# A tanh-attention kernel: softmax denominators as four 32-column products, and a new order of VectorE's steps behind them

## The reference

```python
def proj(W, bias):
    y = jnp.tanh(states @ W + bias)
    return y.reshape(b, s, h, d).transpose(0, 2, 1, 3)     # h = 16 heads, d = 64
q, k, v = (proj(Wq, bq), proj(Wk, bk), proj(Wv, bv))
alpha = jnp.einsum('bhqd,bhkd->bhqk', q, k) / jnp.sqrt(jnp.float32(d))
causal = jnp.tril(jnp.ones((s, s), dtype=bool))
alpha = jnp.where(causal, alpha, jnp.finfo(jnp.float32).min)
alpha = jax.nn.softmax(alpha, axis=-1)
ctx = jnp.einsum('bhqk,bhkd->bhqd', alpha, v)
ctx = ctx.transpose(0, 2, 1, 3).reshape(b, s, h * d)
return jnp.tanh(ctx @ Wo + bo)
```

## Time and profile before

| | |
|---|---|
| median of 3 runs | 1631.6 us (1628.72 to 1643.32) |
| the profiled execution | 1633.24 us, its span 1631.4 us |
| busy: TensorE | 1551.1 us (95%) |
| busy: VectorE | 1419.4 us (87%) |
| busy: ScalarE | 1227.8 us (75%) |
| busy: GpSimd | 461.1 us (28%) |
| mean granted TensorE clock | 0.991 of full |

### The profile page before, as it was taken

One profiled execution on the slowest core, in us unless ns is written; L12 is line 12 of the kernel. 1 busy time (PEld: TensorE's weight loads), 2 busy tenths in 40 slices (PEclk: granted clock), 3 DMA queues, 4 the chain that ended last, 5 costly groups with the idle time before them and its releaser, 6 DMA issues.

```text
span 1631.4 us, 38607 instructions
## 1 busy us (share of the span) xinstructions
PE 1551.1 (95%) x14806; PEld 701.8 (43%) x14806; DVE 1419.4 (87%) x2102; ACT 1227.8 (75%) x1698; POOL 461.1 (28%) x563
## 2 busy tenths in 40 slices
PE   7899999999999999998899999999999999989996
PEld 4344444444444444445333333333333333466774
DVE  6777778888888888998899999999999999397888
ACT  4667666677666676664798999899989999666776
POOL 3311112222333323334135242324332432120004
PEclk9999999999999999999999999999999999899998
DMA  5311001111011110001112000200030000000001
GB/s 146 73 39 40 30 30 40 39 37 39 21 39 39 37 39 34 26 3 33 34 41 53 15 14 15 53 14 15 19 82 19 15 28 2 1 8 8 14 14 52
DMA packets 46606, 52.98 MB, mean 32 GB/s; under 512 B 9279, under 2 KB 33551, under 8 KB 46482
## 3 DMA queue, kind: packets, MB, share of 16 engines
q1 hardware_dynamic: 45584, 50.05, 10.5%
q10 hardware_dynamic: 898, 1.22, 0.3%
HBM read 15.07 MB, written 10.49 MB: 16 GB/s over the span
## 4 chain that ended last, share of the span: by engine, by line
PE 63%; DVE 22%; ACT 10%; issue 3%; POOL 1%; ACTq 0%; POOLq 0%; DVEq 0%
DVE arena L2408 16%; PE psum L590 15%; PE psum L571 12%; ACT arena L2164 7%; PE psum L1916 5%; PE psum L533 5%; PE psum L1547 5%; PE psum L1514 4%; PE psum L608 3%; PE psum L1927 3%; PE psum L628 3%; PE psum L1902 1%; PE psum L553 1%; PE psum L554 1%; PE psum L555 1%
## 5 line engine op out<-in xcount | busy, mean ns | idle before, releaser
L2408 DVE TENSOR_REDUCE arena<-psum 128x2 f32<-128x1024 f32 x490 | 565.7, 1214 | 11.1 <-PE psum L1927 9.8
L2164 ACT ACTIVATE arena<-psum 128x512 f32<-128x512 f32 x980 | 519.6, 600 | 52.0 <-PE psum L1902 46.1
L755 ACT ACTIVATE arena<-psum 128x2048 f32<-128x2048 f32 (+1 forms) x160 | 274.0, 1713 | 229.0 <-PE psum L571 228.9
L1916 PE MATMUL psum<-arena 128*32 128x256 f32 x4096 | 329.2, 393 | 1.4 <-ACT arena L2184 0.2
L859 POOL TENSOR_SCALAR_AFFINE_SELECT arena<-arena 128x512 f32<-128x512 f32 (+1 forms) x160 | 152.7, 972 | 508.7 <-ACT arena L755 508.7
L590 PE MATMUL psum<-arena,hs 128*64 128x512 f32 (+3 forms) x1536 | 283.0, 496 | 0.2 <-POOL arena L859 0.2
L1902 PE MATMUL psum<-arena 32*128 32x512 bf16 x1024 | 255.9, 385 | 1.3 <-ACT arena L2164 0.4
L571 PE MATMUL psum<-arena 64*128 64x512 f16 (+3 forms) x2304 | 215.0, 324 | 2.1 <-DVE arena L907 1.6
L1927 PE MATMUL psum<-arena 32*128 32x512 bf16 x980 | 189.9, 384 | 21.0 <-DVE arena L2408 13.1
L907 DVE TENSOR_TENSOR arena<-arena 128x1024 f16<-128x1024 f32 x64 | 78.4, 1226 | 101.4 <-ACT arena L734 101.4
L590 PEld LDWEIGHTS psum<-arena,hs 128*64 128x64 f32 x1536 | 95.9, 136 | 141.5 <-issue 125.2
(11 more groups left out here) (222 smaller groups left out, 2160.1 us busy)
## 6 DMA issues: line engine op xcount, KB each, us to landing
arena<-arena SPq DMA_DIRECT2D x30, 512.0 KB, 2.9
arena<-arena SPq DMA_DIRECT2D x46, 128.0 KB, 2.2
arena<-latent_q SPq DMA_DIRECT2D x64, 64.0 KB, 2.0
arena<-latent_k SPq DMA_DIRECT2D x64, 64.0 KB, 2.0
arena<-arena SPq DMA_DIRECT2D x60, 64.0 KB, 2.2
X<-in_L_attn_states SPq DMA_DIRECT2D x4, 512.0 KB, 4.4
latent_q<-arena SPq DMA_DIRECT2D x16, 96.0 KB, 2.3
latent_k<-arena SPq DMA_DIRECT2D x16, 96.0 KB, 2.3
```

Of the source, the lines that this page charges most:

```text
L755: nc.scalar.activation(probs[g], SC[:, :, 0:WIDTH[g]], ACT.Exp, scale=DH ** -0.5).then_inc(exp_done, 1)
L1916: last = nc.tensor.matmul(OT[ROWS * c:ROWS * (c + 1), h * HALF // 2:(h + 1) * HALF // 2], v_cols[par][:, kt, 2 * pr + i, :], e_probs[u % 4 ...
L2164: nc.scalar.activation(e_probs[u % 4][:, i * HALF:(i + 1) * HALF], ring(n, u, i), ACT.Exp, scale=KD ** -0.5).then_inc(e_done, 1)
L2408: nc.vector.tensor_reduce(half_tops[:, kh, qt, 2 * pr:2 * pr + 2], src.rearrange("p (i c) -> p i c", i=2), AX.X, ALU.max).then_inc(top_don ...
```

## The change

- `denominators`: each of the four products (head s, half of the queries) takes 32 columns of `ones` and writes a group of 32 partitions of its own, all at the same 512 columns of PJ. The semaphore is raised once, by 2, behind the last.
- `read_denominators`: one transpose of 512 columns in place of two.
- `invert`: writes the inverses of a group of partitions into both halves of `rden_col`.
- `share` (new): four copies of 32 partitions x 16 elements bring to each head's other group of partitions the inverses that it lacks.
- VectorE's order: `add_output(i-2)` now stands ahead of `share` and `spread(i-1)`, where `spread` stood between the first and the second addition of group 3.
- denT is half as long.

```diff
--- before.py
+++ after.py
@@ -366,7 +366,7 @@
         qk_end = a1b.at
         assert qk_end == SUMS_AT
         sums = [a1b.take(2 * S).rearrange("p (s q) -> p s q", s=2) for _ in range(2)]
-        denT = a1b.take(S)
+        denT = a1b.take(HALF)
         rden_col = a1b.take(S // 32)
         ctxT = [a1b.take(S) for _ in range(2)]
         ctx_hi = [a1b.take(S // 2, F16) for _ in range(2)]
@@ -397,6 +397,8 @@
         tile_tanh, tile_stats, tile_pow, tile_normed, tile_added, tile_reset = (
             sem("tile_tanh"), sem("tile_stats"), sem("tile_pow"), sem("tile_normed"), sem("tile_added"), sem("tile_reset"))
         PAIR_DMAS = 3
+        QB = HALF // 32
+        INVERSE = 6
         SUM_LO, SUM_HI = 4, 7
 
         NORM_FROM = PAIRS + 2
@@ -602,12 +604,12 @@
                     pe.wait_ge(tanh_done, 4 * (n + 2) + 4)
                 pe.wait_ge(sum_lo, SUM_LO * (n + 1))
                 pe.wait_ge(sum_hi, SUM_HI * (n + 1))
-                for half in range(2):
-                    now = slice(half * HALF, (half + 1) * HALF)
-                    for s in range(2):
-                        last = nc.tensor.matmul(PJ[s * DH:(s + 1) * DH, now], ones, sums[par][:, s, now],
-                                                start=True, stop=True, skip_group_check=True)
-                    last.then_inc(den_done, 1)
+                for c in range(4):
+                    s, half = c // 2, c % 2
+                    last = nc.tensor.matmul(PJ[ROWS * c:ROWS * (c + 1), 0:HALF], ones[:, 0:ROWS],
+                                            sums[par][:, s, half * HALF:(half + 1) * HALF],
+                                            start=True, stop=True, skip_group_check=True)
+                last.then_inc(den_done, 2)
 
             def output(n, par):
 
@@ -921,24 +923,32 @@
 
             def read_denominators(n):
 
-                for half in range(2):
-                    dve.wait_ge(den_done, 2 * n + half + 1)
-                    now = slice(half * HALF, (half + 1) * HALF)
-                    nc.vector.transpose(denT[:, now], PJ[:, now]).then_inc(den_read, 1)
+                dve.wait_ge(den_done, 2 * n + 2)
+                nc.vector.transpose(denT, PJ[:, 0:HALF]).then_inc(den_read, 2)
 
             def invert(n):
                 dve.wait_ge(den_read, 2 * n + 2)
-                nc.vector.reciprocal(rden_col, denT.rearrange("p (b c) -> p b c", c=32)[:, :, 0]).then_inc(rden_ready, 1)
+                v = denT.rearrange("p (b c) -> p b c", c=32)[:, :, 0].unsqueeze(1).to_broadcast([P, 2, QB])
+                nc.vector.reciprocal(rden_col.rearrange("p (h b) -> p h b", h=2), v).then_inc(rden_ready, 1)
+
+            def share(n):
+
+                dve.wait_ge(rden_ready, INVERSE * n + 1)
+                for c in range(4):
+                    half, other = c % 2, c ^ 1
+                    now = slice(half * QB, (half + 1) * QB)
+                    nc.vector.tensor_copy(rden_col[ROWS * other:ROWS * (other + 1), now], rden_col[ROWS * c:ROWS * (c + 1), now]
+                                          ).then_inc(rden_ready, 1)
 
             def spread(n):
-                dve.wait_ge(rden_ready, 2 * n + 1)
+                dve.wait_ge(rden_ready, INVERSE * n + 5)
                 if not at_least(n, 1):
                     dve.wait_ge(wo_split, 3)
                 nc.vector.transpose(rden.rearrange("p (b c) -> p b c", c=32),
                                     rden_col.unsqueeze(2).to_broadcast([P, S // 32, 32])).then_inc(rden_ready, 1)
 
             def scale_ctx(n, par):
-                dve.wait_ge(rden_ready, 2 * n + 2)
+                dve.wait_ge(rden_ready, INVERSE * (n + 1))
                 dve.wait_ge(out_copied, n + 1)
                 nc.vector.tensor_tensor(ctxT[par], ctxT[par], rden, ALU.mult).then_inc(ctx_scaled, 1)
 
@@ -1039,14 +1049,15 @@
                     states_lo(dve, 1, PJ)
                     state_moments(dve, 3)
                 hi_third(i, par, 0)
-                if at_least(i, 1):
-                    spread(i - 1)
                 hi_third(i, par, 1)
                 hi_third(i, par, 2)
                 if at_least(i, 2):
                     add_output(i - 2)
                 else:
                     states_lo(dve, 2 + i, PJ)
+                if at_least(i, 1):
+                    share(i - 1)
+                    spread(i - 1)
                 if norm:
                     norm_tile(t)
                     add_tile(t)
@@ -1090,6 +1101,7 @@
             read_denominators(N1 - 1)
             invert(N1 - 1)
             quads_ahead(dve, 2, 3)
+            share(N1 - 1)
             spread(N1 - 1)
             scale_ctx(N1 - 1, 1)
             quads_ahead(dve, 3, 4)
```

## The result

| | before | changed |
|---|---|---|
| median (20 runs each) | 1632.95 us (1628.13 to 1643.32) | 1642.78 us (1635.47 to 1646.97) |
| ratio, 95% interval | | 1.0052 (1.0037 to 1.0067) |
| profiled span | 1631.4 us | 1641.0 us |

The changed kernel is slower than before, by half a per cent, and outside the range of the prediction. Over all executions of before that ran beside the experiments, the median is 1628.6 us at a mean clock of 0.995 (12 executions) and 1639.4 at 0.986 (22).

A forecast was written before the change was run, and what follows sets the result against it. TensorE looked busiest, but GpSimd's mask, then VectorE's scaling, would limit the gain. Terms -3.8 + 4.0 - 1.2 - 1.3 = -2.3 took the profiled 1633.24 to 1630.9 us, 1629 us as median; range 1617 to 1640 us.

The forecast's parts named there:

- Four products beside each other: TensorE's denominators: four products run concurrently instead of two and two, shrinking the stage by 0.82 us.
- What of it counts: the mask: TensorE's context 3 then waits for GpSimd's mask, so gains are 0.48 us per early pair (3.8 us), 0.1 us later.
- Output added first: VectorE's output addition starts at about 324.3 instead of 325.59; the values' wait goes, returning late pairs to 22.30 us.
- 0.1 us for uncertainty: Late pairs: allowance for the uncertain start of VectorE's output addition, added to the rounding's start.
- What is late next: VectorE's scaling comes after addition, copies and spreading; ScalarE's context rounding waits for it, with 0.79 us spare before.
- X, the four copies: VectorE's four copies of inverses, 32 x 16 elements each: taken as 0.7 us, between 0.3 and 0.85 us.
- The first mask in the way: GpSimd's group 0 mask goes ahead of VectorE's scaling and delays it by 0.45 us.
- The sum of the late pairs: Pairs 10 to 30: period 22.65 us against 22.45, +4.0 us over twenty pairs, bounds -5 to +11 us.
- the spare behind the rounding: ScalarE, from context rounding to the queries' tanh that releases TensorE's next projection: about 0.1 us of spare.
- Pair 1: TensorE's wait for L228 shortens as the transpose moves and the product shrinks: -1.2 us, bounds 0 and -1.9.
- The end: Last denominators: shorter product stage and earlier addition, less 0.7 us for copies: -1.3 us in all, bounds 0 and -2.5.
- The rival that called it (scaling becomes the bound, 1636 us): Late pairs: copies plus mask make scaling the bound, 23.0 us a pair, 1636 us; chance of slower 0.15.

The follow-up runs named there:

- the run with the mask in two: Changed kernel with context 3 waiting only for the first pass of group 3's mask, its last key tile for the second: 1626.19 us, ratio 0.9956.
- the order alone: Kernel before with only the spreading transpose moved behind the output's addition, two-and-two products, no copies: 1626.49 us, ratio 0.996.
- the old products in the cured order: Changed kernel with scaling ahead of tile steps, context 3's mask wait split, and all 32 pairs' denominators as before, no copies: 1628.99 us, ratio 0.9982.

## Why the prediction was wrong, and where it was right

Forecast 1629.0 us, no change, range 1617 to 1640; measured 1642.78. By its own steps:

- *Four products beside each other.* Right: 1.06 us instead of 1.89, 0.83 saved (0.82 worked out).
- *What of it counts: the mask.* Right. Early pairs gained 3.7 us over eight (3.8), context 3 waits 0.49 us for the mask, and the run with the mask in two takes the wait away. With it early pairs run at 21.58 us, 0.72 under before, so 0.1 us of the 0.82 is held by something else.
- *Output added first.* Right in kind: the values' wait is gone, and the order alone brings the late period to 22.31 (22.30). The addition starts later than I gave it: 0.2 to 0.3 us behind the output's end (320.20 against 318.38 + 1.51 = 319.89), of which 0.17 is "issue"; VectorE's sums before it end at 320.03. The forecast had it start as the product ends, its 0.1 us for uncertainty counted in.
- *What is late next.* Right in kind: scaling, then rounding, which waits 0.66 us in each late pair.
- *X, the four copies.* Mis-sized: 0.76 us for four, and the overlap is lost at both ends (from the addition's start to the spreading's it takes 322.25 - 320.20 = 2.05 us, where an addition with overlap takes 1.14), so about 0.9 against 0.7. That is just past the upper end I gave, 0.85. The Trainium skill (VectorE: DVE Perf Modes, "Two Vector instructions with no wait between them") has each copy wait for the one before it since the partitions change; the trace agrees, 0.19 us from copy to copy against some 0.08 for the small statistics.
- *The first mask in the way.* The mask does go first. I charged 0.45 us on the scaling; the trace shows it on the tile's L1011 instead, 0.34 to 0.43 us (0.68 and 0.77 in alternate pairs, 0.34 alone).
- **The sum of the late pairs is the first step that failed**, in size: +4.0 us forecast, +7.0 measured, 22.80 us a pair instead of 22.65. X came out 0.2 us longer and the addition's start 0.3 us later. Together with the smaller terms that is some 0.45 us over my sizes from the output's end to the rounding, but the period is only 0.15 us over. So the spare behind the rounding, which I set at 0.1 us, was also mis-sized, about 0.4 us (an estimate from that difference).
- *Pair 1.* Right: -1.1 us (-1.2).
- **The end is the step that failed most**: -1.3 us forecast; measured +1.0 from start 30 to 31 and +6.6 behind it. It counted the copies at 0.7 us and looked at nothing that runs beside them. In the end they fall on GpSimd's clears, which the trace of before shows in the same place. There they leave the addition at its 1.22 us, but they hold the tile's L1001 behind it, 1.06 us instead of 0.34, and that was the sign to read:

```profile
752.51 1.22 DVE L920 TENSOR_TENSOR acc<-psum,acc 128x1024 f32<-128x1024 f32 x1
752.78 1.84 POOL L2385 MEMSET arena<- 128x1024 f32 x2
...
753.64 1.06 DVE L1001 TENSOR_SCALAR arena<-arena 128x128 f32<-128x128 f32 x1
```

The copies lose 1.7 us there; moving the clears gives 1.6 of it back. The forecast gain of 1.3 us would be missing even so: with the clears moved TensorE's first pause is still 1.77 us against 0.26 in before, since copies and spreading now stand between the addition and the scaling, and the stretch to the first reduction is 43.3 us against 41.9 (with 1.7 us more of clock time lost). The rest of the profiled 6.6 us goes with TensorE's clock, which stood at half for some 20 us there and for which the forecast had no term; by the table above the stretch grows by such an amount in every kernel whose clock is lost there, copies or none. What makes the clock fall more often in the changed kernel (13 of 20 executions; before between 5 of 17 and 15 of 25) is open: the first pause of TensorE was my cause, and filling it did not help; the second pause, 3.23 us in that run against 2.4 in before, was not filled. The 1.0 us between starts 30 and 31 is open too: with the order alone the stretch is 23.57 us, near before, but with the old products in the cured order it is 24.20.

At a like clock the two kernels are 5.6 us apart at 0.993 (1635.6 and about 1630, two executions of each); by the profiled executions, 2.0 lie ahead of start 30. At 0.985 they are within a microsecond (1643.7, nine executions, and 1643.0, two). The rival that called it (scaling becomes the bound, 1636 us) had the mechanism and nearly the price of the pairs, 23.0 us for 22.8, but it too missed the end.

## What to carry to other kernels

Before moving or adding a small operation on VectorE, list what GpSimd runs at its new place in every phase, the last one too: the same four copies cost 0.76 us in 31 pairs and 2.45 in one. Follow a late step round until it comes back to itself: in a loop across engines (here scaling to mask to addition to scaling) savings can add, and a saving that a later wait seems to swallow can come back when that wait is cut, as 0.6 us of the new products and their copies did. And when a change is judged by a few microseconds, look at the clock of each execution before the medians.

## What I had not expected

- VectorE copies of 32 x 16 elements stop for GpSimd's clears, which only write (2.45 against 0.76 us); reciprocals of the same shape don't (1.07 and 1.07 us).
- TensorE's granted clock falls to half at the end of the phase even when the longest pause there is filled: at about 762 us, within a pause of 3.33 us, in the changed kernel; with that pause filled at about 778 us, behind the next one of 3.23 us. It then stood there for some 20 us in both. Kernels with the same results, run side by side, have a low mean clock in 2 of 12 or in 12 of 12 executions.
- Two waits in the same pair, 0.49 us on TensorE and 0.66 on ScalarE, could be taken out one by one; each gave some 0.54 us, and both together 1.10.
